# Feed-forward chunks grouped in pairs in the 8-head layers, a last feed-forward part by chunks, and another order of a row norm

## What is computed

```python
x = x + _L1_attn_ref(_layernorm(x), Wqkv, Wo)          # 16 heads, causal
x = x + _L1_ffn_ref(_layernorm(x), wqkv, ..., w2, b2)   # two layers, below

def _layer(x, wqkv, qs, ksc, wo, lg, lb, w1, b1, w2, b2):
    q, k, v = jnp.split(shift_token(x) @ wqkv, 3, axis=-1)
    q, k = rotary_xpos(l2norm(q) * qs, l2norm(k) * ksc)
    o = local_attention(q, k, v)      # 8 heads of 64, window of 128 rows and the one before
    x = x + o @ wo
    h = norm(shift_token(x)) * lg + lb
    a, g = jnp.split(h @ w1 + b1, 2, axis=-1)      # 682 units each
    return x + (a * gelu(g)) @ w2 + b2
```

## Time and profile before

| | us |
|---|---|
| median of three runs | 2541.02 (2537.96 to 2543.17) |
| profiled execution, its own time | 2549.92 |
| its span in the trace | 2548.2 |
| PE busy | 2288.1, 90% of the span |
| DVE, ACT, POOL busy | 1544.3, 1312.5, 921.1 |
| 16-head attention | from about 602 to 1217 |
| two layers | 1217.6 to the end |

### The profile page before, as it was taken

How to read it: one execution, slowest core, us unless ns; L and a number is a source line. 1 busy time by engine, 2 the same in 40 slices (tenths; PEclk the granted TensorE clock), 3 DMA queues, 4 the chain that set the end, 5 groups by cost and what they waited for, 6 DMA issues and landing times.

```text
span 2548.2 us, 45050 instructions
## 1 busy us (share of the span) xinstructions
PE 2288.1 (90%) x15746; PEld 1738.7 (68%) x15746; DVE 1544.3 (61%) x4777; ACT 1312.5 (52%) x3211; POOL 921.1 (36%) x1363
## 2 busy tenths in 40 slices
PE   7999599996788887878699999999999999999997
PEld 4666499995445363544577777777777777777776
DVE  5555522224666747564667677776777776777764
ACT  1112033332655755465555675656755666566662
POOL 2221122212434433332544344333544544434441
PEclk9999699998788988878899999999999999999998
DMA  3222311112002010100200000000001000000000
GB/s 131 100 99 83 129 36 36 36 34 83 18 3 67 3 54 16 34 35 11 88 9 18 18 1 18 17 18 18 35 26 62 26 10 18 26 26 26 1 18 25
DMA packets 75937, 96.39 MB, mean 38 GB/s; under 512 B 6114, under 2 KB 69091, under 8 KB 75459
## 3 DMA queue, kind: packets, MB, share of 16 engines
q1 hardware_dynamic: 70786, 81.89, 9.6%
q0 software_dynamic: 3408, 9.31, 1.3%
q10 hardware_dynamic: 1520, 2.31, 0.3%
HBM read 62.69 MB, written 30.28 MB: 36 GB/s over the span
## 4 chain that ended last, share of the span: by engine, by line
PE 27%; DVE 9%; ACT 8%; issue 5%; POOL 3%; DMA 0%; DVEq 0%; SPq 0%; POOLq 0%; ACTq 0%
PE l_free L2122 4%; PE l_free L2124 3%; PE l_free L2123 3%; PE l_out L2237 3%; PE l_score L2197 2%; POOL l_probs L1632 2%; PE l_turned L2218 2%; DVE l_work L1801 2%; DVE l_probsT L1727 2%; DVE l_u_low L1807 2%; PE l_turned L2122 1%; PE l_turned L2124 1%; PE l_turned L2123 1%; ACT l_probs L2005 1%; PE l_turned L2171 1%
## 5 line engine op out<-in xcount | busy, mean ns | idle before, releaser
L1632 POOL TENSOR_SCALAR l_probs<-l_probs,l_rinv 128x256 f32<-128x256 f32 (+1 forms) x512 | 222.2, 453 | 229.6 <-DVE l_rinv L1787 229.5
L1062 DVE CUSTOM_DVE_ANT_0 c_raw<-cbank,c_later 128x256 f32<-128x256 f32 (+3 forms) x512 | 218.6, 487 | 73.6 <-PE cbank L1249 72.9
L2005 ACT ACTIVATE l_probs<-l_probs,l_nmax 128x256 f32<-128x256 f32 (+1 forms) x512 | 240.0, 474 | 26.0 <-DVE l_nmax L1782 26.0
L1165 ACT ACTIVATE c_cprobsT<-cbank 128x384 f32<-128x384 f32 (+1 forms) x384 | 180.9, 525 | 90.5 <-PE cbank L1275 90.4
L1782 DVE CUSTOM_DVE_ANT_0 l_probs<-l_score,mask,l_inv 128x256 f32<-128x256 f32 (+1 forms) x512 | 200.0, 447 | 28.4 <-PE l_score L2197 27.7
L2122 PE MATMUL l_free<-l_part,l_w_high 128*128 128x512 f32 x384 | 166.1, 432 | 9.6 <-DVE l_probsT L1727 6.5
L2122 PE MATMUL l_free<-l_wqkv_high,l_yT 128*128 128x512 f32 x384 | 159.0, 414 | 1.8 <-DVE l_part L1706 1.8
L1765 DVE COPY l_probsT<-l_turned 128x512 f32<-128x512 f32 (+1 forms) x128 | 79.8, 624 | 132.6 <-PE l_turned L2218 81.8
L964 POOL TENSOR_SCALAR_AFFINE_SELECT c_cprobsT<-c_cprobsT 128x256 f32<-128x256 f32 x256 | 99.3, 410 | 160.5 <-ACT c_cprobsT L1165 158.2
L2123 PE MATMUL l_free<-l_yT,l_w_high 128*128 128x512 f32 x384 | 153.1, 399 | 0.0
L2124 PE MATMUL l_free<-l_part,l_w_low 128*128 128x512 f32 x384 | 152.8, 398 | 0.0
(11 more groups left out here) (263 smaller groups left out, 5849.9 us busy)
## 6 DMA issues: line engine op xcount, KB each, us to landing
w<-in_W1T SPq DMA_DIRECT2D x8, 1024.0 KB, 7.9
w<-in_W2T SPq DMA_DIRECT2D x8, 1024.0 KB, 11.4
ys_d<-m_y SPq DMA_DIRECT2D x39, 128.0 KB, 1.7
xn_d<-a_prods SPq DMA_DIRECT2D x8, 512.0 KB, 3.1
c_came<-x_d SPq DMA_DIRECT2D x8, 512.0 KB, 5.0
y_d<-c_raw SPq DMA_DIRECT2D x8, 512.0 KB, 3.7
early_rows<-y_d SPq DMA_DIRECT2D x8, 512.0 KB, 3.7
l_came<-y_d SPq DMA_DIRECT2D x8, 512.0 KB, 3.9
```

Source lines behind the costliest of these rows:

```text
L1062: last = dve.tensor_tensor_reduce(raw[:, CHUNKS - NS + s, h * 2 * P:h * 2 * P + wide], score_place("scores", u, s)[:, h * 2 * P:h * 2 * P ...
L1165: act.activation(probsT[s][:, c % 2, i, k0:k0 + w], turned_place(j, s)[:, 0:w], ACT.Exp).then_inc(probs_ready[s], 1)
L1632: pool.tensor_scalar(a, a, rinv[:, j, r, h:h + 1], 1.0, ALU.mult, ALU.mult).then_inc(normed, 1)
L2005: act.activation(a, a, ACT.Exp, bias=nmax[:, j, r, h:h + 1], scale=-1.0, accum_out=rsum[:, j % 2, r, h:h + 1])\
```

## The change

There are three edits.

1. `HIDDEN_AT`: the twelve chunks stood at two each in steps 0 to 2 and one each in steps 3 to 8. Now they stand at two each in steps 0, 1, 2, 3, 5 and 7, and steps 4, 6 and 8 have none. DVE's and ACT's copies move with them.
2. The last pass of the two layers, on ACT and DVE: copy, gelu or gating, and the parts now go group by group. In every half, `contract` waits for one group at a time in its first tile, in place of all six.
3. `first_norm`: DVE now normalises stream 0 between the sum and the statistics of stream 1.

```diff
-                        for s in range(NS):
+                        def whole_rows(s):
                             if trip:
                                 dve.wait_ge(x_in[s], trip * 16)
...
+                        whole_rows(0)
+                        row_measure(0)
+                        whole_rows(1)
+                        row_norm(0)
+                        row_measure(1)
+                        row_norm(1)
...
-        HIDDEN_AT = ((0, 1), (2, 3), (4, 5), (6,), (7,), (8,), (9,), (10,), (11,))
+        HIDDEN_AT = ((0, 1), (2, 3), (4, 5), (6, 7), (), (8, 9), (), (10, 11), ())
...
-                for n in range(HALVES + 1):
+                for n in range(HALVES):
...
+                for c in range(UC):
+                    take_out(HALVES - 1, 2 * c + 1)
+                    gated(HALVES - 1, c, alone=True)
+                    if c:
+                        low_units(HALVES - 1, c - 1)
+                low_units(HALVES - 1, UC - 1)
+                for tile in range(NT):
+                    add_rows(HALVES - 1, tile)
...
+                for c in range(UC):
+                    take_out(HALVES - 1, 2 * c)
+                    gelu(HALVES - 1, c, alone=True)
+                    if c:
+                        high(HALVES - 1, c - 1)
+                high(HALVES - 1, UC - 1)
...
                     if first == 0:
                         pe.wait_ge(w2_split, layer + 1)
-                        pe.wait_ge(u_ready[s], pair * UC + UC)
...
                         for c in range(UC):
+                            if t == 0:
+                                pe.wait_ge(u_ready[s], pair * UC + c + 1)
```

More of the change, by code:

```diff
@@ L1009, in first_norm, with row_measure, row_norm @@
                             dve.tensor_tensor(rows[s][:], came[s][:], rows[s][:], ALU.add).then_inc(x2_ready[s], 1)
+                        def row_measure(s):
                             dve.wait_ge(x2_ready[s], trip + 1)
                             row_stats(dve, chain, var_ready[s], lambda t: [rows[s][:, t, :]], stats[s], mv[s], ve[s])
-                        for s in range(NS):
+                        def row_norm(s):
                             for ins in normalised_rows(dve, rstd_ready[s], trip + 1, lambda t: [rows[s][:, t, :]], mv[s], rstd[s],
@@ L1793, in take_out, with gated @@
                     dve.tensor_copy(uT[s][:, c, :], free_bank[k % 3][:]).then_inc(a_out[s], 1)
-                def gated(n, c):
+                def gated(n, c, alone=False):
                     s, pair, layer, _ = place(n)
@@ L1798, in gated @@
                         dve.wait_ge(b1_in, 16 * (layer + 1))
+                    if alone:
+                        dve.wait_ge(a_out[s], pair * UC + c + 1)
+                    elif c == 0:
                         dve.wait_ge(a_out[s], pair * UC + UC)
@@ L2030, in take_out, with gelu @@
                     act.activation(gate[s][:, c, :], free_bank[k % 3][:], ACT.Copy).then_inc(g_out[s], 1)
-                def gelu(n, c):
+                def gelu(n, c, alone=False):
                     s, pair, layer, _ = place(n)
@@ L2035, in gelu @@
                         act.wait_ge(b1_in, 16 * (layer + 1))
+                    if alone:
+                        act.wait_ge(g_out[s], pair * UC + c + 1)
+                    elif c == 0:
                         act.wait_ge(g_out[s], pair * UC + UC)
```

## The result

| | us |
|---|---|
| before, median of four runs | 2540.17 (2537.96 to 2543.17) |
| after, median of four runs | 2587.95 (2582.89 to 2592.88) |
| ratio, 95% interval | 1.0182 (1.0168 to 1.0196) |
| profiled execution after, its time and its span | 2586.93, 2585.2 |

The changed kernel is 1.8% slower, 46 us by the ratio; the forecast was 2581, 1.6%. The busy line of the page answers the earlier trace rows: PE is busy 8 us less, the others as long as before, in 37 us more span.

A forecast was written before the change was run, and what follows sets the result against it. PE was taken to set the time in the layers. The terms 40.5 + 8.7 - 9.8 + 0.7 = +40.1 us took the profiled 2549.9 to 2590.0, as a median 2581 us, 1.6% slower; 8-in-10 range 2566 to 2612.

The forecast's parts named there:

- The loop of edit 1: Layers' empty steps: PE waits for POOL 1.46, 0.60 and 1.46 us; 2.78 us a half, 41.7 in 15 halves.
- That nothing behind step 8 takes up the delay: End of each half: what follows hangs on unit 5's outputs through ACT, so 2.78 us pass on in full.
- The term for half 9: Unit 6's transposes already wait 1.24 us for POOL's weight split; that lies under the new wait: -1.2 us.
- the 40.5 of the sum: Layers, edit 1: total +40.5 us, with bounds of +20 and +75.
- Edit 2: Last pass: going by groups removes PE's wait before the second product, -9.8 us (-7 to -10.5).
- the 0.7 in the sum for the finer waits: `contract` in the halves: waiting for one group at a time costs +0.7 us in the sum.
- Edit 3: Norm in the 16-head attention: 2.4 us late in the first pair, 2.1 in three later ones; +8.7, between 0 and 12.
- the first pair: First pair of the norm: the second stream's normalising begins at 622.9 instead of 620.5, 2.4 us late.
- the cover isn't needed (a): Rival in the layers: POOL's result comes in time, edit 1 saves 10.7 us, kernel 11 us faster at 2530; 5%.
- the clock falls in most halves (b): Rival in the layers: new gaps lower PE's clock, +25 us if once in each half, median 2606; 17%.

The follow-up runs named there:

- Halving POOL's work: Changed kernel with POOL scaling only the first 128 of the 256 probabilities of the wide units: 2565.75 us, ratio 1.0097.
- moving the inverse: Changed kernel with DVE's inverse of the next unit ahead of the copy of the transposed probabilities in steps 3, 5 and 7: 2565.21 us, ratio 1.0095.
- the single gap in step 4: Kernel before with chunk 7 alone moved from step 4 to step 3, so only step 4 is empty: 2557.41 us, ratio 1.0061.
- the candidate with the rows first: Kernel before with edit 2, inverses ahead on DVE, and PE's transposes of the next half's rows ahead of unit 6's outputs: 2533.17 us, ratio 0.9968.
- edit 2 alone: Kernel before with only the last pass by chunks and the finer waits of `contract`: 2530.76 us, ratio 0.9954.
- edit 1 alone: Kernel before with only the new grouping of the twelve chunks: 2586.90 us, ratio 1.0169.
- edits 1 and 2: Changed kernel with the norm in the old order, so without edit 3: 2577.68 us, ratio 1.0151.
- edit 3 in the first pair alone: Kernel before with DVE's new norm order in the first pair only, later pairs in the old order: 2544.93 us, ratio 1.0014.
- both candidates: Rows first (2533.17 us), and kernel before with edit 2, inverses ahead, only steps 4 and 6 empty, outputs ahead of scores there (2526.76 us).

## Why the prediction was right, point by point

**The loop of edit 1** was right in every link. 3.61, 3.18 and 3.61 us were forecast from transposes to transposes, and 3.61, 3.18 and 3.60 came. The waits were to be 1.46, 0.60 and 1.46 and are 1.39, 0.53 and 1.39, each 0.07 less: PE's own stretch reaches to 2.22, where I took the 2.15 to the start of a chunk. In the half that ends with the outputs at 1610.27, the six distances from transposes to transposes changed by +1.17, -0.14, +1.38, -0.99, +1.65 and -0.16 us, where +1.23, -0.13, +1.40, -0.99, +1.40 and -0.13 were forecast; the one large miss holds the 0.20 that PE loses behind the narrow wait. A half: 2.78 forecast, 2.86 measured. Halving POOL's work and moving the inverse show that the loop is the cause, not only that it stands there.

**That nothing behind step 8 takes up the delay** was argued from ACT's copy and table load. It held: the single gap in step 4 cost its full 1.07 a half, and the candidate with the rows first showed the ACT and DVE chain that carries it.

**The term for half 9 was wrong, also in sign.** I took 1.2 us off, as if the new wait and POOL's wait for its split weight lay on each other. In the trace they add in part: POOL starts on unit 6 only when its part of the weight is done, and PE waits 2.22 us. From the first scores of half 9 to the transposes of unit 6 are 39.75 us after 37.39, 2.36 more, where half 3 has 2.83 more: 0.5 came off, not 1.2. And behind that wait the clock falls, which I had not put into this term. The rows are PE's timeline there, after:

```profile
2026.63 0.80 PE L2248 MATMUL l_turned<-ident,l_probs 64*128 64x64 f32 x16 [2.22 <-POOL l_probs L1642]
2027.37 1.97 PE L2267 MATMUL l_out<-l_probsT,l_v 128*64 128x128 f32 x16
2030.13 1.97 PE L2267 MATMUL l_out<-l_probsT,l_v 128*64 128x128 f32 x16 [0.79 <-ACT l_oT L2044]
2032.03 1.97 PE L2168 MATMUL l_free<-ident,early_rows 128*128 128x128 f32 x8
```

Outputs take 1.97 in place of 1.09, and from these transposes to the output projection are 7.94 us, where the kernel before has 5.21: 2.7 more. From the outputs of unit 6 in half 8 to those in half 10 are 174.07 us after 166.44, 7.6 more and not the 5.7 of two steady halves. Against that, from the first transposes of the layers to the outputs of unit 6 in half 1 it is only 2.0 more, 0.9 less than a steady half gives; half 0 has spells at the lower clock in both traces, of different lengths. 15 x 2.86 = 42.9 with 1.9 more and 0.9 less is 43.9, and the layers have +44.1, 3.6 above the 40.5 of the sum.

**Edit 2** was to bring 9.8 and brought 9.2 with the clock up at the start of the last pass in both. What I had not seen is that the 38.27 us from which I started held about 2 us of the lower clock, so that the same edit shows as 11.3 in these two profiles. No run shows the 0.7 in the sum for the finer waits: with edit 2 alone the 16 halves take 1287.79 us against 1288.07.

**Edit 3** was to cost 8.7 and cost 6.9 alone (7.9 against the kernel without it). The delay at each place is as worked out: POOL's second power comes 4.48 us behind the first (733.64 to 738.12), where 4.6 was forecast, and PE's outputs wait 2.48 for the banned keys. For the first pair, projections start 8.98 us behind the first power (605.24 to 614.22) in place of 7.13, a delay of 1.85, not 2.4. But a spell at half the clock goes with that delay, which the sum had at nothing: the first four products of that projection take 2.55 to 3.47 us in all five traces with the new order in the first pair and 1.88 in all nine with the old one. Pair 1 takes 124.7 to 128.4 us in the former and 121.8 to 122.4 in the latter. From there to the end of the stage the clock adds and takes back some us from execution to execution.

**The whole**: 44.1 + 6.9 - 9.2 = 41.8 with the measured sizes, 40.1 as forecast, 46.2 (42.7 to 49.8) by the ratio. Both lie just below. That the forecast is within 2 us of the 41.8 is in part luck: it was 3.6 too low for edit 1 and 0.6 for edit 2, and too high by 1.8 for edit 3 and by 0.7 for the finer waits. Between 1 and 8 us of the whole are in no term; the stages before and in the 16-head attention vary by that much between executions, and I can't tell from one profile of each kernel how much of it the new order of the norm brings about.

**The rivals.** That the cover isn't needed (a) is refuted by the waits. That the clock falls in most halves (b) did not come: with waits of 1.39 and then 0.79 it stayed at 1.00. A fall that the kernel before has not came once, in half 9, behind 2.22 us. The Trainium skill, "TensorE: Matmul & The Clock Gate", section on PE-mode transpose, says that a transpose "doesn't count as PE-busy the same way". By that rule the emptied steps should have looked idler than they are; the steady halves show no fall, and no run here separates transposes from other work.

## What to carry to other kernels

Work that stands between two uses of a loop over other engines is its cover: before it is grouped elsewhere, add up the loop link by link (here transposes, copy, inverse, scaling: 3.61 us against 2.22 of PE's own), and do the same for the next loop behind it, since taking away the first wait brought back two thirds as others. A wait on the busiest engine is a gain only if it ends the stretch that it stands in; here 0.79 us on PE were slack ahead of ACT and DVE. And when a profile is the base of a sum, look at the granted clock of each stretch that is to change, so that a chance spell at the lower level isn't booked as a gain.

## What the runs showed of the hardware

The clock's fall in half 9 goes with the length of the wait. It fell to 0.50, 1.2 GHz, in the three traces with a wait of 2.21 or 2.22 us (changed kernel, edit 1 alone, edits 1 and 2), and stayed at 1.00 in the eleven others, with 0.79 to 1.45. The closest pair is the changed kernel and the one with POOL's half work, since PE's program is the same in both and the waits are 2.22 and 1.42. This is the window around it in the first and then, at the same work, in the second:

```profile
2027.00:2034.00 7.00, 6.21 (x54) 5.06 (x51) 2.11 (x3) 4.41 (x6) 1.72 (x4) 0.51 0.00 0
```

```profile
2012.60:2017.10 4.50, 3.71 (x59) 3.16 (x56) 1.36 (x3) 4.02 (x8) 1.42 (x4) 1.00 0.00 0
```

But the length of one wait doesn't decide it everywhere. The output projection of half 15, behind a wait of 1.96 or 1.97 us, took 5.41 us in eleven traces and 3.72, at full clock, in two (POOL's half work, and edit 3 in the first pair alone).

The second surprise is the reach of such spells. At the start of the last pass, behind the same wait of 3.01 us, the clock was up in nine executions and down for 3 to 6 us in five others. The new last pass took 26.95 us in four of them, 28.5 in one and 29.6 in both candidates, with the same instructions; the old one took 36.0 to 36.3, 38.3 or 39.3. By this spell alone two executions can differ by 3 us.
